# Linear attention one tile at a time, in the slots of the latent attention's next two pairs

## The reference, cut to what matters

```python
x = x + _L0_xattn_ref(ctx_1024, _layernorm(x), ...)      # 16 heads of 64; each batch: 64 latents, 256 + 64 keys
x = x + _L0_attn_ref(_layernorm(x), Wq, bq, Wk, bk, Wv, bv, gamma, beta)
x = x + _L0_ffn_ref(_layernorm(x), w_gate, w_up, w_down) # hidden 768, integer weights / 127
...                                                      # second layer: attention, a scanned cell, 8 experts
def _L0_attn_ref(x, ...):                                # 16 heads of 16, each batch of 64 rows by itself
    q = relu(x @ Wq.T + bq); k = relu(x @ Wk.T + bk); v = x @ Wv.T + bv
    kv = einsum('bnhd,bnhp->bhdp', k, v); k_sum = k.sum(axis=1)
    denom = maximum(einsum('bnhd,bhd->bnh', q, k_sum), 1e-6)
    y = einsum('bnhd,bhdp->bnhp', q, kv) / denom + x
    return (y - mean(y)) / sqrt(var(y) + 1e-5) * gamma + beta
```

## Time and profile before

| | |
|---|---|
| time, median of 3 runs | 2062.15 us (2060.33 to 2063.23) |
| the profiled execution: its time, its span | 2063.35 us, 2061.6 us |
| PE, PEld, DVE, ACT, POOL busy | 98%, 88%, 58%, 55%, 29% of the span |
| `latent_attention` | start to about 824.1 us |
| `linear_feed` | 826.0 to 1025.3 us (next stage's first matmul at 1027.07) |
| `decoder` | to the end |
| granted TensorE clock, mean | 0.997 |

### The profile page before, as it was taken

One profiled execution on the slowest core, in us unless ns is written; L12 is line 12 of the kernel. 1 busy time (PEld: TensorE's weight loads), 2 busy tenths in 40 slices (PEclk: granted clock), 3 DMA queues, 4 the chain that ended last, 5 costly groups with the idle time before them and its releaser, 6 DMA issues.

```text
span 2061.6 us, 46366 instructions
## 1 busy us (share of the span) xinstructions
PE 2017.7 (98%) x18705; PEld 1809.6 (88%) x18705; DVE 1192.4 (58%) x3581; ACT 1124.9 (55%) x2556; POOL 601.5 (29%) x652
## 2 busy tenths in 40 slices
PE   7999999999999999899899999999999999999998
PEld 6999999999999999477778888788999999999998
DVE  6756565656565554677568898726939624233311
ACT  5656566666666655333367877554454444444443
POOL 1311132111111110132212122244444444444444
PEclk9999999999999999999999999999999999999999
DMA  4111311111111100100031110101010101101000
GB/s 166 60 30 50 98 43 38 42 38 43 37 43 37 53 17 1 47 1 1 10 91 41 35 32 14 43 1 62 1 41 1 42 1 42 41 1 42 1 11 31
DMA packets 55987, 73.60 MB, mean 36 GB/s; under 512 B 7968, under 2 KB 41568, under 8 KB 55648
## 3 DMA queue, kind: packets, MB, share of 16 engines
q1 hardware_dynamic: 55776, 70.65, 10.7%
HBM read 62.45 MB, written 2.16 MB: 31 GB/s over the span
## 4 chain that ended last, share of the span: by engine, by line
PE 45%; DVE 2%; ACT 2%; issue 1%; POOL 0%; POOLq 0%; DVEq 0%; ACTq 0%
PE bank L83 20%; PE bank L1132 17%; PE bank L1053 2%; PE bank L1040 1%; PE bank L1068 1%; ACT att_p L1238 1%; PE bank L1098 1%; PE bank L1009 1%; ACT att_pt L1243 1%; PE bank L1079 0%; POOL right_h L963 0%; DVE dec_room L140 0%; ACT att_kt L1230 0%; PE bank L1091 0%; DVE att_vz L1385 0%
## 5 line engine op out<-in xcount | busy, mean ns | idle before, releaser
L963 POOL TENSOR_TENSOR right_h<-right_hr,right_h 128x512 fp32r<-128x512 f32 x256 | 342.0, 1336 | 417.2 <-ACT right_hr L1285 417.2
L1284 ACT ACTIVATE right_h<-bank,dec_b 128x512 fp32r<-128x512 f32 x256 | 176.2, 688 | 389.6 <-PE bank L83 366.5
L83 PE MATMUL bank<-lat_wv,lat_kv_t 128*128 128x256 f32 (+1 forms) x1728 | 258.9, 300 | 0.7 <-issue 0.7
L83 PE MATMUL bank<-lat_kv_t,lat_qk 128*128 128x320 f32 x1536 | 253.5, 314 | 0.0
L83 PEld LDWEIGHTS bank<-lat_kv_t,lat_qk 128*128 128x128 f32 x1536 | 226.4, 188 | 7.7
L83 PEld LDWEIGHTS bank<-lat_wv,lat_kv_t 128*128 128x128 f32 x1728 | 222.9, 190 | 6.8 <-issue 1.1
L2299 ACT ACTIVATE lat_p<-bank,lat_neg_max 128x320 f32<-128x320 f32 x256 | 136.3, 532 | 145.3 <-DVE lat_neg_max L2431 144.7
L83 PE MATMUL bank<-dec_xt,dec_lo 128*128 128x512 f32 x512 | 200.4, 391 | 0.0
L1285 ACT ACTIVATE right_hr<-bank,dec_b 128x512 f32<-128x512 f32 x256 | 174.5, 682 | 0.0
L1132 PE MATMUL bank<-dec_hi,right_h 128*128 128x256 f32 x1024 | 161.6, 279 | 1.2 <-POOL right_h L963 1.2
L1132 PE MATMUL bank<-moe_hi,right_h 128*128 128x256 f32 x1024 | 161.9, 280 | 0.4 <-POOL right_h L963 0.4
(11 more groups left out here) (332 smaller groups left out, 3976.3 us busy)
## 6 DMA issues: line engine op xcount, KB each, us to landing
raw_w<-in_L_ffn_W SPq DMA_DIRECT2D x16, 1024.0 KB, 6.3
lat_ctx_raw<-in_ctx SPq DMA_DIRECT2D x16, 512.0 KB, 3.8
right_ctx_raw<-in_ctx_turned SPq DMA_DIRECT2D x16, 512.0 KB, 3.7
lat_kv_f<-in_ctx_turned SPq DMA_DIRECT2D x15, 512.0 KB, 3.8
lat_ctx_raw<-gate_rows SPq DMA_DIRECT2D x15, 512.0 KB, 3.9
lat_kv_t<-lat_lt SPq DMA_DIRECT2D x32, 128.0 KB, 3.4
out_x<-x_sb SPq DMA_DIRECT2D x4, 512.0 KB, 2.9
x_sb<-in_x SPq DMA_DIRECT2D x1, 1792.0 KB, 14.9
```

The source lines that it names most:

```text
L83: mm = pe.matmul(out, lhs(a, k), rhs(b, k), start=first and k == 0 and n == 0, stop=last and k == KD - 1 and n == 2)
L963: pool.tensor_tensor(h[:, g % 2, 1, :], hr[:, g % 2, :], h[:, g % 2, 0, :].bitcast(F32), ALU.subtract).then_inc(h_lo, 1)
L1284: act.activation(h[:, n % 2, 0, :], h_bank[n % 2][:, :], ACT.Relu, bias=bias).then_inc(h_hi, 1)
```

## The change

Linear attention leaves the stage behind and goes into `latent_attention`, one tile at a time. Tile i is finished by the latent attention in pair i; its rows are normalised and turned, and its queries, keys and values computed, in slots 3 to 6 of pair i + 1; its states, contexts, second normalisation and sum in slots 1 to 6 of pair i + 2. Tiles 0 to 13 are done there wholly; of tile 14 the states and contexts are left, and tile 15 is left whole. The second stage, now `feed_forward`, does these between the first pieces of gate and up; it keeps three of the twelve matmuls of `keep_awake`, starts with feed-forward of chunk 0, and goes through the chunks one after the other. Besides:

- the large part of the gate and up weights (`up_high`) is made by ACT in the last pair, in the room of Wq, and their small part in the stage behind; `wd` is split there as before;
- the 14 later latents are normalised two at a time (`xl_now`) at slot 0 of odd pairs, not all at once in pair 1, and a transfer per couple (`latents_now`) falls away;
- the statistics of the next context, which stood in two halves in slot 7 and slot 0, stand wholly in slot 7, and `turn_columns` goes from slot 1 to slot 0;
- POOL scales `room` in nine pieces, one a pair from pair 4 on;
- the loads of Wq, Wk, Wv, the biases, gamma and beta stand behind the loads of the first stage's weights on SP's queue.

The diff, cut to its core (what is left out of `linear_feed` is the removed chunked form of the same operations):

```diff
+class TileAttention:
+    def pe_rows(self, pe, i, bank):
+        pe.wait_ge(self.l_xn, i + 1)
+        for kd in range(KD):
+            mm = pe.transpose(bank[:, kd * P:(kd + 1) * P], self.xn[:, i % 2, kd * P:(kd + 1) * P], self.ident[:, :])
+        mm.then_inc(self.rows_psum, 1)
+    def pe_queries(self, pe, i, bank):
+        pe.wait_ge(self.xt_ready, i + 1)
+        for m in range(KD):
+            for kd in range(KD):
+                mm = pe.matmul(bank[:, m * P:(m + 1) * P], self.wq[:, kd, m * P:(m + 1) * P], self.xt[:, kd, :], ...
+    def pe_keys_values(self, pe, i):
+        for kd in range(KD):
+            mm = pe.matmul(self.own_bank[:, :], self.xt[:, kd, :], self.wkv[:, kd, :], start=kd == 0, stop=kd == KD - 1)
+    def pe_states(self, pe, i, bank):          # 4 matmuls, 64 rows x 129 columns
+    def pe_contexts(self, pe, i):              # 4 matmuls, 136 columns
+    def dve_stats(self, dve, i):
+        self.norm_l.row(dve, self.x_sb[:, i, :], i)
+        self.norm_l.close(dve, i)
+    def dve_keys_values / dve_states / dve_contexts / dve_y_stats / dve_scale / dve_ffn_row ...
+    def act_rows / act_turned / act_queries / act_keys ...
+    def pool_shift / pool_beta / pool_shift_of_ffn ...
@@ extras(pair, s)
+            if s == 1:
+                steps.append(("xs", pair - 2, 0))
+            if s == 4:
+                steps.append(("xr", pair - 1, 0))
+            if s == 5:
+                steps.append(("xq", pair - 1, 0))
@@ tensor, slot
+                if s == 3 and here >= 2:
+                    pe.wait_ge(o_lo, NU // 2 * here + 1)
+                    tile.pe_contexts(pe, here - 2)
...
+                        if s == 4 and here >= 2:
+                            pe.wait_ge(tile.ctx_step, 4 * (here - 2) + 4)
+                        if s == 6 and here >= 1:
+                            pe.wait_ge(tile.v_ready, here)
                         weigh(c, back, hp // 2)
@@ scalar, slot
+                    if s == 3:
+                        tile.act_rows(act, here - 1)
+                    if s == 4:
+                        tile.act_turned(act, here - 1, bank_of("xr", c, off - 1, 0))
+                    if s == 5:
+                        tile.act_queries(act, here - 1, bank_of("xq", c, off - 1, 0))
+                    if s == 6:
+                        tile.act_keys(act, here - 1)
@@ vector, slot
-                if i >= 1 and more and s == 0:
-                    context_rows(i + 1, (2, 3))
...
                 if s == 7 and i + 2 < NT:
-                    context_rows(i + 2, (0, 1))
+                    context_rows(i + 2, range(4))
+                    norm_c.finish(dve, (i + 2) * norm_c.steps)
...
                 if s == 1 and (not first or off == 1):
                     residual(c, off - 1)
+                    if i >= 2:
+                        tile.dve_states(dve, i - 2, bank_of("xs", c, off - 2, 0))
+                    dve.wait_ge(x_done, i)
+                    tile.dve_stats(dve, i - 1)
+                if s == 3 and i >= 2:
+                    tile.dve_contexts(dve, i - 2)
+                    tile.dve_y_stats(dve, i - 2)
+                if s == 5 and i >= 1:
+                    tile.dve_keys_values(dve, i - 1)
+                if s == 5 and i >= 2:
+                    tile.dve_scale(dve, i - 2)
+                if s == 6 and i >= 2:
+                    tile.dve_ffn_row(dve, i - 2)
@@ feed_forward, tensor
+            tile.pe_states(pe, LAST - 1, tile_bank)
+            keep_awake(2)
+            turn_ffn(0)
+            keep_awake(1)
+            for h in range(NH):
+                gate_up(0, h)
+                ...                            # contexts of tile 14, then tile 15, behind h = 0, 1, 2, 4, 5
```

More of the change, by code:

```diff
@@ L478, in _ @@
+            for c in range(NCH):
+                if c >= 1:
+                    for h in range(NH):
+                        gate_up(c, h)
+                if c + 1 < NCH:
+                    turn_ffn(c + 1)
+                down_two(c)
+                for i in range(2, PER):
+                    down(c, i)
         @block.scalar
         def _(act):
-            def rows_apply(c):
-                if c == Ahead.CHUNKS:
-                    act.wait_ge(l_shift, 1)
-                for i in range(PER):
-                    t = PER * c + i
-                    act.activation(xn[:, c % 2, i, :], x_sb[:, t, :], ACT.Identity, bias=shift_l[:, t:t + 1],
-                                   scale=norm_l.rstd[:, t:t + 1]).then_inc(l_xn, 1)
@@ L563, in _ @@
-            for h in range(NH):
-                gate(NCH - 1, h)
-                high(NCH - 1, h)
+            for i in range(PER):
+                ffn_apply(0, i)
+            act.wait_ge(f_xn, 1)
+            act.activation(table[:, :], fn[:, 0, 0:1], ACT.Silu)
+            ffn_turned(0)
+            tile.act_rows(act, LAST)
+            for c in range(NCH):
+                for h in range(NH):
+                    gate(c, h)
+                    high(c, h)
+                    if (c, h) == (0, 1):
+                        tile.act_turned(act, LAST, tile_bank)
+                    if (c, h) == (0, 2):
+                        tile.act_queries(act, LAST, tile_bank)
+                        tile.act_keys(act, LAST)
+                    if c + 1 < NCH and 1 <= h <= PER:
+                        ffn_apply(c + 1, h - 1)
+                if c + 1 < NCH:
+                    ffn_turned(c + 1)
@@ L631, in rows_stats @@
-            def rows_stats(c):
-                for i in range(PER):
-                    norm_l.row(dve, x_sb[:, PER * c + i, :], PER * c + i)
             def ffn_low(c):
@@ L1970, in _ @@
             load_weight(3)
+            tile.load(nc, sp, w)
             def load_ahead():
@@ L1987, in couple @@
                     i = 2 * c + off
-                    if off == 1 and not last:
-                        latents_now(c)
                     if not last or off == 0:
@@ L2001, in _ @@
             sp.wait_ge(ahead_in, 48)
-            sp.wait_ge(ahead_whole, 64)
+            sp.wait_ge(tile.loads, tile.LOADS)
             sp.wait_ge(ctx_in, 16 * NT)
@@ L2471, in slot @@
                         norm_x.finish(dve, 0)
-                if first and off == 1 and s < 7:
-                    if s == 0:
+                if off == 1 and s == 0 and not last:
+                    if first:
                         dve.wait_ge(norm_x.rstd_ready, 1)
-                    for t in (2 * s + 2, 2 * s + 3):
+                    for t in (i + 1, i + 2):
                         latents_apply(t)
@@ L2569, in perceiver @@
             k.near = Near(nc, k.near_room)
-            linear_feed(nc, k, x_sb, banks, w)
+            feed_forward(nc, k, x_sb, banks, w)
             k.end_stage()
```

690 lines of the change are left out of this document (311 added, 379 removed).

## The result

The changed kernel takes 2092.7 us, the median of 4 runs (2089.9 to 2094.1), against 2062.7 for the kernel before on the same chip: a ratio of 1.0146, 95% interval 1.0128 to 1.0164, 30.0 us slower. The forecast was 2080, range 2063 to 2092. The sign and most of the mechanism were right. The sum gave +18.4, so the size was 11.6 us short, and the time lies just above the range. One place that the forecast put at nothing, slot 2, cost 9.6 us.

The account below looks back on a forecast made before the run. PE was taken to bound the latent stage, with no gap there. Matmuls 62.4 plus new waits 34.9 less 78.9 from the stage behind gave +18.4 us, hence 2081.8 profiled and a forecast median of 2080, range 2063 to 2092.

Parts of the forecast that it names:

- Matmuls, 62.4: Latent stage: linear attention's matmuls are paid in full on PE, 62.4 us more (60 to 66).
- Slot 0, 12.0: Statistics ahead of slot 0's maxima delay `weigh`: 1.58 us in odd pairs, 0.13 in even ones, seven times each.
- Slot 4, 16.7 of waits: DVE's contexts and statistics of y delay slot 4: 1.23 us in even pairs (9.8 with pair 15), 1.15 in odd (6.9).
- Slot 1, 0.55: Odd pairs: the states' second bank, that of "w", waits for DVE's residual, 0.55 us, seven times, 3.9.
- Slot 5, 2.3: "v" waits for the turned rows' bank until ACT has copied it: 0.15 us, 15 times, 2.3.
- Slots 2 and 6 hold.: No new wait in slots 2 and 6: DVE's additions end 2.3 and 1.7 us into them, soon enough for `weigh`.
- The stage behind, -78.9: The second stage, without most of linear attention, takes 120.4 us against 199.3: 78.9 less (75 to 82).
- the chain is hidden: Rival: in the latent stage DVE's additions fall where PE would not notice, new waits vanish, -16.5 us, 2046; chance 0.10.
- The clock rival: Waits every few slots lower the granted clock in the latent stage, 34 us at most, 2114; chance 0.04.

Follow-up runs that it names:

- e4: Changed kernel with the edits of e1, e2 and e3 together: 2055.6 us, ratio 0.9970 to the kernel before.
- e1: Changed kernel with the context's statistics in two halves again (slots 7 and 0) and the turning of columns back in slot 1: 2068.4 us.
- e6: Kernel before with only the context's statistics moved as in the change (all in slot 7, turning in slot 0): 2075.5 us against 2062.5.
- e3: Changed kernel with GpSimd's context normalisation issued behind the shift of the tile's rows, other engines' orders kept: 2082.2 us.
- e2: Changed kernel with the addition of the rows and the statistics of y moved on DVE from slot 3 to slot 4, behind its normalisations: 2078.3 us.
- e7: e4 with the states put ahead of the turned latents in slot 1 of odd pairs, so their second bank differs: 2051.6 us.
- 11: e4 with the bank-dealing list no longer counting the never-issued queries of a seventeenth pair: 2052.2 us.
- e12: e4 plus the edits that helped: those of experiment 7, e7 and 11: 2047.0 us, ratio 0.9923 to the kernel before.
- experiment 7: e4 with tile 15's row normalisation behind the first silu and DVE's split of `wd` later, in chunk 0 of the stage behind: 2050.8 us.

## Why the prediction was right, and where it was short

- **Matmuls, 62.4.** Right in sum. In e4 the latent stage, from its first energies to the last output projection, is 69.7 us longer than before, of which 3.6 (slot 1) and 2.5 (pair 15's slots 4 to 6) are waits: 63.6. Keys and values took 1.31 and not 1.85, but 0.4 is paid by the energies behind them; the contexts cost 0.82, of which 0.17 is a longer pause ahead of them.
- **Slot 0, 12.0.** Right: 1.55 for 1.58 forecast, by e1 and e6. Pair 1, which I gave the same price, cost 2.8, and 1.56 in e3, where GpSimd's operations stand later.
- **Slot 4, 16.7 of waits.** The mechanism was right in both kinds of pair (e2), the size a little high: by the slots' lengths e2 takes away 0.96 and 1.04 (PE's idle time was 0.90 and 0.83) where 1.23 and 1.15 were forecast. Pair 15's two bank waits were not seen.
- **Slot 1, 0.55.** Right in place and cause, `w`'s bank (e7), 0.5 measured.
- **Slot 5, 2.3.** This wait did not come: no row of PE waits for the turned rows' bank there, and a steady pair's slot 5 is 2.17 to 2.26 longer, the 0.89 and 1.31 of its matmuls. Only pair 15 waits, 0.97 us, for another bank (11).
- **"Slots 2 and 6 hold."** This is the step that failed. Slot 6 held. Slot 2 cost 9.6 us, since DVE's additions ended 3.3 and not 2.3 us into it. They were priced by rows in which such a small operation takes 0.16; that the change moves POOL's context normalisation nearly eight microseconds forward, on to them, was not worked out at all. e3 shows it to be the cause: it takes 8.9 us out of slot 2, and 10.5 off the time.
- **The stage behind, -78.9.** The mechanism was right, the size 4.2 short. Chunk 0 took 44.5 for 42.3, chunks 1 and 2 27.0 each for 26.3, and chunk 3 was 0.3 longer. Within chunk 0 a lower clock is worth more than the 2.2: some 2.5 us in the head of the stage and 1.6 behind the wait of 1.97 (last section); at full clock chunk 0 would have been shorter than forecast. The bound given for this term, 75, held it but for 0.3.
- **Rivals.** That the chain is hidden came true for none of it as changed; e4, 0.3% faster than before, shows that it could be had with the same matmuls on other places in DVE's list. With every new wait hidden the sum was -16.5 us; e12 has -15.3, though not by the same terms, since in its profiled execution, the fastest of its five, the latent stage costs 63 us and the stage behind saves 82. The Trainium skill (Perfetto Trace Analysis, Optimization Strategy) says that interleaving stretches with different bounding engines may gain: the change as it was made, 30.0 us slower, did not bear that out, and e12 does. The clock rival fell: 1.00 in the latent stage, with 46 waits in it.
- The range was too narrow by the one unknown it left out: each term had bounds for its own rows, none for a neighbour's work moving beside it.

## What to carry to other kernels

When a step moves earlier on one engine, follow what it releases: here four statistics, put one slot forward on VectorE, let GpSimd begin 16 operations nearly eight microseconds sooner among the slots, on top of VectorE's. Where the bounding engine has no slack, ask of each list on each helper engine at which time its next *needed* operation starts, and put additions behind it, not ahead: moving three groups, without one instruction less, gave 37 us where the whole change had cost 30. And where banks are dealt out by a list, steps that are counted but never issued still shift them.

## What the hardware showed that I had not expected

- VectorE operations with two operands in SBUF, of one column (L121, L122), took 0.49 us beside GpSimd's operations of 128 columns (0.42 us each) and 0.15 without them, in all records between 203 and 818 us (11 of each line in the changed kernel, 10 in e3). The addition of 256 columns at 945.63 (experiment 7) took 1.38 and not 0.42 us, beside one GpSimd operation from 945.44 to 946.73. The statistics L113, the one-column tensor-scalar L126 and the maxima beside them kept their time. A wider tensor-scalar did not: the normalisation of the weights, 320 columns and one operand tile in SBUF, took 0.39 us alone, 0.46 to 0.82 beside GpSimd in 24 of its 256 records in the changed kernel, and 1.49 once in e1 (pair 8, row below). The Trainium skill (SBUF — State Buffer, Who interferes with whom) says that a VectorE instruction with two SBUF inputs contends with a GpSimd instruction that reads SBUF, through an exclusive lock on a shared pair of ports, and that on trn2 a reduction never contends; the rows agree. With that rule, and with GpSimd's new place worked out, slot 2's wait could have been looked for.

```profile
488.03 1.49 DVE L2442 TENSOR_SCALAR lat_p<-lat_p,lat_rinv 128x320 f32<-128x320 f32 x1
```

- The granted clock in the head of `feed_forward` differs from one profiled execution to another with the same instructions. From the states of tile 14 to the first `gate_up`, behind the same pause of 2.02 us, it was 0.64 in the changed kernel (7.89 us, the window 931.58:939.47 above), and 0.74 in e4, whose window is this:

```profile
895.42:902.11 6.69, 6.06 (x22) 3.29 (x23) 4.72 (x5) 4.63 (x8) 0.00 (x0) 0.74 0.67 199
```

In e2, which has the same instructions there, it was 1.00:

```profile
918.16:923.59 5.43, 4.37 (x23) 2.44 (x23) 4.72 (x5) 4.42 (x8) 0.00 (x0) 1.00 0.62 177
```

So 1.3 to 2.5 us of a difference between two profiles can lie there, and 1.6 more behind the wait of 1.97 in chunk 0, where the clock was 0.68 or 1.00 (7). Neither goes with the other: in e7 the head had 0.75 and the clock behind the wait 1.00. What decides them was not tried.
